# Gated linear attention layer: the two additions into the residual rows on VectorE instead of GpSimd

## The reference, cut to what matters

```python
xn  = layernorm(x)
q, k, v, g = xn @ Wq, xn @ Wk, xn @ Wv, xn @ Wg
gk  = log_sigmoid(xn @ Wgk1 @ Wgk2 + bgk2) / 16
o   = gla_scan(q, k, v, gk)           # h = h * exp(gk) + k v^T;  o = q h, 4 heads
y   = x + (rmsnorm(o) * g * sigmoid(g)) @ Wo
h   = leaky_relu(layernorm(y) @ W1 + b1, 0.01) ** 2
y   = y + h @ W2 + b2                 # what the layer returns
x   = layernorm(x + y)                # around the layer
```

## Time and profile before

| what | value |
|---|---|
| median of 3 runs | 3316.36 us (3308.28 to 3322.06) |
| the profiled execution, its own time | 3312.32 us |
| span of its profile (first to last instruction) | 3310.2 us |
| layer that is changed | from about 30 to 745 us of the span |
| busy over the span | PE 81%, DVE 51%, ACT 42%, POOL 14% |
| mean granted TensorE clock | 0.872 |

### The profile page before, as it was taken

The page is one execution under the profiler, slowest core; times in us unless marked ns, Lnnn a source line. Parts: engine busy times, 40 slices in busy tenths (PEclk is TensorE's granted clock), DMA queues, the critical chain, the costliest instruction groups (busy, mean ns, idle before and its releaser), DMA issues. The chain is left out here.

```text
span 3310.2 us, 33970 instructions
## 1 busy us (share of the span) xinstructions
PE 2674.6 (81%) x12536; PEld 1656.6 (50%) x12536; DVE 1684.8 (51%) x3451; ACT 1378.1 (42%) x1853; POOL 459.3 (14%) x411
## 2 busy tenths in 40 slices
PE   2888888865888888879994887784688888887998
PEld 1656666542333333355562545453366666665655
DVE  3455555534556665616432778785544444532222
ACT  2333333311555555612223565551366666661121
POOL 0111111110000000000463132232201111000000
PEclk9788888876999999969896989987799989997999
DMA  2000000005333332140246111111200000001000
GB/s 66 7 13 13 13 13 13 7 7 140 54 59 61 63 66 52 27 139 4 52 64 136 52 52 65 39 69 44 57 13 26 26 26 26 13 7 64 13 19 20
DMA packets 126037, 140.94 MB, mean 43 GB/s; under 512 B 38752, under 2 KB 108656, under 8 KB 125872
## 3 DMA queue, kind: packets, MB, share of 16 engines
q1 hardware_dynamic: 113968, 124.07, 13.9%
q0 software_dynamic: 11904, 14.69, 2.7%
HBM read 77.89 MB, written 35.39 MB: 34 GB/s over the span
## 5 line engine op out<-in xcount | busy, mean ns | idle before, releaser
L929 DVE TENSOR_REDUCE xattn_tops<-region 128x2 f32<-128x1024 f32 x256 | 305.6, 1219 | 146.1 <-PE region L735 146.0
L867 ACT ACTIVATE xattn_probs<-region 128x1024 f32<-128x1024 f32 x256 | 256.1, 1022 | 154.1 <-PE region L724 153.3
L2107 PE MATMUL region<-psi_fT 128*128 128x512 f32 x512 | 245.5, 624 | 21.7 <-DVE psi_low L2341 21.1
L122 PE MATMUL region<-gla_xT,weights_even 128*128 128x512 f32 (+1 forms) x416 | 221.0, 687 | 26.7 <-ACT gla_xT L214 26.7
L724 PE MATMUL region<-xattn_qs,xattn_ks 49*128 49x512 f32 x512 | 125.6, 492 | 85.9 <-DVE xattn_tops L929 54.8
L122 PE MATMUL region<-mamba_xT,weights_odd 128*128 128x512 f32 x320 | 169.5, 681 | 5.1 <-DVE mamba_xh L1904 5.1
L2107 PEld LDWEIGHTS region<-psi_fT 128*128 128x128 f32 x512 | 97.1, 200 | 125.4 <-issue 100.6
L122 PEld LDWEIGHTS region<-gla_xT,weights_even 128*128 128x128 f32 (+1 forms) x416 | 82.8, 208 | 151.0 <-issue 119.3
L2128 PE MATMUL region<-psi_ctxv,psi_pT 128*128 128x65 f32 x1024 | 137.4, 300 | 20.8 <-issue 19.4
L2128 PEld LDWEIGHTS region<-psi_ctxv,psi_pT 128*128 128x128 f32 x1024 | 136.3, 216 | 30.0 <-issue 30.0
L751 PE MATMUL region<-xattn_probs,xattn_va 128*32 128x512 f32 x1024 | 144.0, 630 | 1.1 <-ACT xattn_o_T L895 1.1
(11 more groups left out here) (493 smaller groups left out, 5430.4 us busy)
## 6 DMA issues: line engine op xcount, KB each, us to landing
weights_even<-mamba_cs SPq DMA_DIRECT2D x32, 512.0 KB, 4.8
xattn_qs<-xattn_qhi SPq DMA_DIRECT2D x128, 64.0 KB, 2.3
xattn_ks<-xattn_khi SPq DMA_DIRECT2D x128, 64.0 KB, 2.3
moe_sums<-moe_picked SPq DMA_DIRECT2D x9, 512.0 KB, 7.8
gla_x<-in_x SPq DMA_DIRECT2D x8, 512.0 KB, 3.8
x_after_gla<-gla_res SPq DMA_DIRECT2D x8, 512.0 KB, 2.9
xattn_ctxT<-in_ctxT SPq DMA_DIRECT2D x8, 512.0 KB, 4.1
xattn_x<-x_after_gla SPq DMA_DIRECT2D x8, 512.0 KB, 4.1
```

The lines of the kernel that those rows point to most:

```text
L122: last = st.nc.tensor.matmul(o[0:m, i, :], w[:, c, col + i * P:col + i * P + m], rhs[:, c, :], start=c == 0, stop=c == kc - 1)
L867: A_(probs[:, p % 3, a, :, :], st.region(f"k{v}")[:], ACT.Exp).then_inc(st.emptying(f"k{v}"), 1)
L929: V.tensor_reduce(tops[:, n % 2, t, a::2], st.region(f"q{u}")[:], AX, ALU.max).then_inc(st.emptying(f"q{u}"), 1)
L2107: last = mm(o[:, a, :], fT[:, h, 0, t * P:t * P + P], fT[:, h, 1 + a, :], start=True, stop=True)
```

## The change

The first addition, `res = x + b2`, moves from GpSimd's step `xT` to DVE's step `xT`, with its wait for the store; the wait for the load of `x` falls away, since DVE has waited for it in `first`. The second, `res += x`, moves from GpSimd's step `second` 0 to the end of DVE's step `second` 1, behind the four instructions that write `xn`. Signals keep their names. `TT` is `nc.vector.tensor_tensor`, `G` is `nc.gpsimd`.

```diff
@@ DVE @@
                     elif what == "first":
                         norms["first"].apply(dve, Z["x"], Z["xn"]).then_inc(st.sem("xn1"), 1)
+                    elif what == "xT":
+                        if b >= 2:
+                            dve.wait_ge(st.sem("stored"), 16 * (b - 1))
+                        TT(Z["res"][:], Z["x"][:], times(K["b2"], NT), ALU.add).then_inc(st.sem("biased"), 1)
...
                     elif what == "second":
                         norms["second"].apply(dve, Z["x"], Z["xn"]).then_inc(st.sem("xn2"), 1)
+                        TT(Z["res"][:], Z["res"][:], Z["x"][:], ALU.add).then_inc(st.sem("res"), 1)
@@ GpSimd @@
-                    elif what == "xT":
-                        if b >= 2:
-                            pool.wait_ge(st.sem("stored"), 16 * (b - 1))
-                        pool.wait_ge(st.sem(f"x_in{b % 2}"), 16 * (b // 2 + 1))
-                        G.tensor_tensor(Z["res"][:], Z["x"][:], times(K["b2"], NT), ALU.add).then_inc(
-                            st.sem("biased"), 1)
...
                     elif what == "second" and i == 0:
                         norms["second"].gpsimd(pool, nth, K["neg_half"], 1e-5)
-                        pool.wait_ge(st.sem("biased"), b + 1)
-                        G.tensor_tensor(Z["res"][:], Z["res"][:], Z["x"][:], ALU.add).then_inc(st.sem("res"), 1)
```

## The result

The changed kernel takes 3288.4 us (median of 6, 3281.6 to 3290.4) against 3316.8 us before: ratio 0.9915, 95% interval 0.9898 to 0.9932, so 28 us faster (23 to 34). The forecast was 3295 us, 21 us faster. The profiled execution took 3287.1 us, with a span of 3285.4 us: 24.8 us less than before. The last store of the layer is issued at 719.9 us instead of 744.6, and from there to the end of the span it is 2565.5 and 2565.6 us, so all of the difference lies in this layer.

What follows compares the result with a forecast made beforehand. PE is the busiest engine, and the wait the change can touch is for DVE's normalized rows, 27.1 us. Terms of 16.2 + 2.0 + 3 = 21.3 us off 3316.4 give 3295 us, range 3284 to 3307.

Steps and rivals of the forecast that it cites:

- The second addition leaves GpSimd: PE's wait before the transposes of `xT2` falls from 2.70 to 0.67 us, in eight batches: 16.2 us gained.
- The first batch: Without GpSimd's first addition, the first L178 of all is no longer held and PE gets `xn` earlier: 2.0 us gained.
- The seven L570: In the other seven batches L570 ends 2.13 us earlier, but PE takes `on` later without having waited: gain nothing.
- The arrivals on DVE: Both additions, taken as 1.22 us each on DVE, fall into its idle time: cost zero.
- The worst case: DVE's first addition and GpSimd's short instructions exclude each other; L570 ends at 198.1, before 200.43: still no cost.
- The wait for the store: On DVE's queue ahead of L570; the store lands at most 4.1 us after issue, before DVE comes: cost zero.
- The clock: Shorter low-clock stretch behind `xT2`: at most 0.87 us a batch, 0.4 taken, in seven batches 3 us gained.
- rival C: Low-clock stretches behind `xT2` and in front of `out` both vanish: 3280 us, in part 3287; chance 0.1.
- rival D: Scores, `o` and other work run longer at the low clock, up to 1.7 us a batch: 3304 to 3310; chance 0.14.
- A: The terms as summed, waits plus a little from the clock: 3295 us, range 3290 to 3300; chance 0.5.
- B: PE's waits shrink but the clock gives nothing: 3298 us; chance 0.2.
- E: DVE's instructions are long from their place behind a wait for GpSimd, not from its addition: 3316 us; chance 0.03.

Runs made afterwards that it cites:

- first_only: Kernel before with only the first addition moved to DVE, the second staying on GpSimd: 3311.0 us, ratio 0.9994 to the kernel before.
- second_only: Kernel before with only the second addition moved to DVE, the first staying on GpSimd: 3289.0 us, ratio 0.9936 to the kernel before.
- pool_behind: Kernel before with both additions kept on GpSimd, each waiting until DVE's instruction is done: 3292.3 us, ratio 0.9936 to the kernel before.
- no_additions: Changed kernel with each addition replaced by a one-element DVE instruction, so the result is wrong: 3290.6 us, ratio 0.9935 to the kernel before.
- more_first: Changed kernel with four more additions, 4.3 us in all, ahead of DVE's first addition: 3289.0 us, ratio 0.9926 to the kernel before.
- late_1: Changed kernel with one more instruction like L178's ahead of the four that write `xn`: 3304.2 us, ratio 0.9973 to the kernel before.
- late_3: Changed kernel with three more instructions like L178's ahead of the four that write `xn`: 3302.2 us, ratio 0.9961 to the kernel before.

## Why the prediction was right, by its own steps

**The second addition leaves GpSimd, 16.2 us.** Measured 27.1 - 11.1 = 16.0 us. Shown by first_only, second_only and pool_behind: from batch to batch only this overlap matters, and it is an overlap.

**The first batch, 2.0 us.** PE's first transposes came at 37.65 instead of 39.53 us: 1.9 us.

**The seven L570, nothing.** Shown by first_only.

**The arrivals on DVE, nothing.** Shown by no_additions, and more_first for the first. The worst case was the true one, though milder than its 1.22 us: L618 was held for 0.9 us. So had the Trainium skill it (SBUF — State Buffer, Who interferes with whom): a DVE instruction with two SBUF inputs locks out a GpSimd instruction that reads SBUF. `on` was ready at 351.4, 2.6 us before PE took it; I had 2.3. The second is free only behind `xn`: ahead of it, it cost 12 us.

**The wait for the store, nothing.** Right in the time, closer than I had it: in one batch the store took 4.4 us, more than the 4.1 that the rows had as the longest, and L504 waited 0.17 us. In that batch L621, the power, took 3.78 us instead of 2.90 beside L504, and L574 still ended at 191.7, 2.3 us before PE took `on` at 193.97. What a later store would do was not tried.

**The clock, 3 us.** This is the term that was mis-sized. Of the 24.7 us by which the layer is shorter, 17.9 us are the two waits, and 6.8 us are left, for which I had 3. They are what remains of a larger effect. PE's matmuls took 12.6 us less in the layer, at a granted clock of 0.83 for 0.81; the wait ahead of L357 took 6.0 us back (18.0 for 12.0 over the layer), and the other waits of PE changed by 1.2 us at most.

In a usual batch (78.6 us for 82.0) the wait gives 2.0 us, the stretch from `xT2` to `out` 0.75 to 1.0 us, where I had worked out 0.87 as the most, and the work from `out` on 0.65 us. I had put the vanishing of the low stretch in `out` last, in rival C, and argued that it could not be, as the wait before `out` does not shrink. It did not shrink, and the stretch vanished nevertheless; why is not shown. It gave `out` 1.68 us, about the half of 3.5 us that C has, but C counted all of it, and I had not looked at what comes next: there DVE had had only 0.56 us of idle time in front of its copy, so 1.0 us was lost again at L357. One batch in six gave 2.9 us back through a longer low stretch in the scores, as rival D had it. So A, C and D all happened, in different stretches, and that the sum came within 7 us owes something to luck: what `out` gained, what L357 took back and what the long batch cost were all left out of it, and in good part they cancel. B falls, since the clock gave something. Between the profile's 25 us and the medians' 28 lies the spread of single runs.

E falls with pool_behind. Why a batch falls on one pattern of low stretches or another is not settled: late_1 shows that it depends on more than the length of the wait, since the same 1.01 us stood before batches of 78.2 and of 81.8 us.

## What to carry to other kernels

Where a short DVE instruction starts within 0.1 us of a GpSimd instruction and lasts as long as both, suspect that it is being held, as L178 and L570 were here: look at the maximum of its duration, not the mean, and ask whether an engine with nothing else to do waits for it. The cure is to part the two in time, on either engine; then place the moved work behind the signal that others wait for. Then follow the gain to the next wait: here `out` became 1.7 us shorter and 1.0 us of it ended in front of a copy on DVE. A few tenths of a us at such a wait can be worth several times as much or nearly nothing, since the clock of TensorE moves along. A sum of waits gave the sign here, and the size to within 7 us for the change (21 for 28) and 9 us for late_1 (the layer 11.4 us longer for 8 x 0.32 = 2.6 us of waits).

## What the hardware showed unexpectedly

- The hold works both ways: beside DVE's addition GpSimd's 0.20 us instruction takes 1.04 to 1.11 us. But a GpSimd power of 128x16 lets four DVE additions run beside it, in whole or in part, at 1.1 to 1.2 us each, while a GpSimd addition of 128x1024 held DVE's instruction for nearly all of its 2.34 us. The same section of the Trainium skill has the pair of ports locked for the whole instruction; for the addition the trace agrees, for the power it does not.
- 0.32 us more in one wait of a batch of 79 us made the batch 1.1 us longer on average (late_1), while 0.97 us more (late_3) made it 1.2 us longer, in one profiled execution each.
